# Moving one tile in 64 of a row gather from GpSimd to SyncE in a two-layer graph network

## What is computed

```
x_src = x[src]
msg   = sum over r of where(edge_type == r, x_src @ W[r], 0)
cnt   = zeros(nodes, 8).at[dst, edge_type].add(1)
norm  = 1 / max(cnt[dst, edge_type], 1)
out   = segment_sum(msg * norm, dst) + x @ root + bias
```

## Time and profile before

| | us |
|---|---|
| median of 3 runs | 19301.76 |
| lowest, highest | 19297.16, 19303.48 |
| the profiled execution, device time | 19300.3 |
| its span in the profile | 19298.5 |
| GpSimd busy | 13724.0 (71%) |
| TensorE busy, matmul / weight load | 8836.8 (46%) / 7749.4 (40%) |
| VectorE busy | 3708.6 (19%) |
| ScalarE busy | 2928.3 (15%) |

### The profile page before, as it was taken

One profiled execution on the slowest core, in us unless ns is written; L12 is line 12 of the kernel. 1 busy time (PEld: TensorE's weight loads), 2 busy tenths in 40 slices (PEclk: granted clock), 3 DMA queues, 4 the chain that ended last, 5 costly groups with the idle time before them and its releaser, 6 DMA issues. The chain is left out here.

```text
span 19298.5 us, 202733 instructions
## 1 busy us (share of the span) xinstructions
PE 8836.8 (46%) x35275; PEld 7749.4 (40%) x35276; DVE 3708.6 (19%) x4240; ACT 2928.3 (15%) x13902; POOL 13724.0 (71%) x14217
## 2 busy tenths in 40 slices
PE   6565054444544444544444444444544444444443
PEld 2343044444434443444434333433434434444433
DVE  2223921111111111111111211111111111111113
ACT  1001021111111111111111111111111111111111
POOL 1672977777777777777776577777777777777774
PEclk9556555555555555555555655555555555555555
DMA  2122010000000000000000300000000000000001
GB/s 82 53 53 93 15 14 7 7 7 7 7 7 7 7 7 7 7 7 7 7 7 6 66 7 7 7 7 7 7 7 7 7 7 7 7 7 7 7 7 10
DMA packets 659318, 296.37 MB, mean 15 GB/s; under 512 B 351570, under 2 KB 628327, under 8 KB 657917
## 3 DMA queue, kind: packets, MB, share of 16 engines
q0 software_dynamic: 455680, 168.10, 8.0%
q1 hardware_dynamic: 202813, 124.51, 2.6%
q10 hardware_dynamic: 402, 0.09, 0.0%
HBM read 207.97 MB, written 87.17 MB: 15 GB/s over the span
## 5 line engine op out<-in xcount | busy, mean ns | idle before, releaser
L109 POOL DMA_INDIRECT l_rows<-table,l_idx x13312 | 12854.8, 966 | 4628.7 <-issue 4056.0
L1002 PE MATMUL l_ps<-l_rows,l_hot 128*128 x28160 | 6327.3, 375 | 0.0
L1002 PEld LDWEIGHTS l_ps<-l_rows,l_hot 128*128 128x128 f32 x28160 | 6137.8, 330 | 395.1 <-issue 395.1
L999 PE MATMUL l_ps<-l_zero 1*128 1x128 f32 x3520 | 1341.0, 482 | 9041.2 <-issue 9041.2
L982 ACT ACTIVATE l_rows<-l_rows,all_big 128x16 f32<-128x16 f32 x13312 | 2662.7, 292 | 13759.6 <-DMA l_rows<-table,l_idx 13759.3
L999 PEld LDWEIGHTS l_ps<-l_zero 1*128 1x128 f32 x3520 | 873.9, 307 | 9179.8 <-issue 9179.8
L1035 DVE TENSOR_TENSOR all_big<-all_big,l_ps 128x128 f32 x1760 | 507.0, 288 | 13988.1 <-PE l_ps L1002 13988.1
L1041 DVE TENSOR_TENSOR l_hot<-l_ps,all_local 128x1024 f32<-128x1024 f32 x1760 | 2126.9, 1219 | 50.6 <-issue 49.9
L109 POOL DMA_INDIRECT s_rows<-table,s_idx x832 | 785.0, 944 | 320.8 <-issue 251.7
L520 PE MATMUL s_ps<-s_zero 1*128 1x512 f32 x448 | 345.1, 909 | 438.5 <-issue 390.0
L523 PEld LDWEIGHTS s_ps<-s_rows,s_hot 128*128 128x128 f32 x1792 | 373.1, 317 | 140.2 <-issue 140.2
(11 more groups left out here) (173 smaller groups left out, 1682.9 us busy)
## 6 DMA issues: line engine op xcount, KB each, us to landing
l_rows<-table,l_idx POOLq DMA_INDIRECT x13312, 2.3
table<-midt_out SPq DMA_DIRECT2D x49, 512.0 KB
table<-x1t_out SPq DMA_DIRECT2D x48, 512.0 KB, 2.7
table<-ed_out SPq DMA_DIRECT2D x48, 320.0 KB, 2.1
s_rows<-table,s_idx POOLq DMA_INDIRECT x832, 2.6
idx_d<-ed_typ SPq DMA_DIRECT2D x2, 3328.0 KB, 9.4
l_idx<-idx_d SPq DMA_DIRECT2D x208, 32.0 KB, 1.8
ed_typ<-in_edge_type_dram SPq DMA_DIRECT2D x2, 2912.0 KB
```

What stands on the lines that cost most here:

```text
L109: pool.indirect_dma_start(out=out[:, j, :], out_offset=None, in_=table, in_offset=bass.IndirectOffsetOnAxis(ap=idx[:, j:j + 1], axis=0)).t ...
L999: nc.tensor.matmul(sums[g % 2], zero[:, :], zero[:, :], start=True, stop=False, skip_group_check=True)
L1002: last = nc.tensor.matmul(sums[g % 2][:, bass.ds((v % GROUP) * FEAT, FEAT)], hot[:, g % 2, j, :], rows[:, bass.ds(v // GROUP, 1), :].rearr ...
```

## The change

It concerns the two runs of `stage_layer`. GpSimd gathers the first 63 tiles (`BY_POOL`) of each block of 64. The last tile's 128 rows are fetched by SyncE with 128 DMAs of one row (64 bytes) each. Their row numbers come from a small SBUF buffer `row_idx` of two halves, into which SyncE loads one column of `idx1_d` a block ahead; from there they are loaded into registers of SyncE, four at a time, with a minimum of 0 and a maximum of 399,999 (for layer 1; layer 2 has the same number). SyncE's part becomes `turn(i)`: turn 0 is written out ahead of the wait for `started`, turns 1 to 7 are a loop. In it the load of the next row numbers for the whole block stands behind the 128 row DMAs, and loads the list of block n + 12 once block n - 1 has landed. The rows of SyncE count on a semaphore of their own, `rows_in[b]`, and ScalarE waits for both. `idx1_d` gets 832 columns more, filled with the first ones again, so that loads ahead of the last turn have something to read.

```diff
--- before.py
+++ after.py
@@ -41,6 +41,8 @@
 GROUP = 8
 GROUPS = STEPS // GROUP
 RING = 13
+BY_SP = 1
+BY_POOL = SPAN - BY_SP
 RTILES = RING * SPAN
 TURNS = TILES // RTILES
 HOLD = -(-(WINS - 1 + SPAN - 1) // SPAN)
@@ -229,8 +231,9 @@
             sp.wait_ge(wide_read, batches)
             sp.dma_start(env.idx0_d, typ6[:, :]).then_inc(idx_out, 16)
             sp.wait_ge(wide_read, 2 * batches)
-            sp.dma_start(env.idx1_d, typ8[:, :]).then_inc(idx_out, 16)
-            sp.wait_ge(idx_out, 32)
+            sp.dma_start(env.idx1_d[:, TILES:], typ8[:, 0:RTILES]).then_inc(idx_out, 16)
+            sp.dma_start(env.idx1_d[:, 0:TILES], typ8[:, :]).then_inc(idx_out, 16)
+            sp.wait_ge(idx_out, 48)
             sp.wait_ge(tables_back, 96)
             sp.wait_ge(dst_stored, 48)
             for b in range(2):
@@ -922,6 +925,7 @@
         rows = s.sb("rows", [P, RTILES, FEAT])
         idx = s.sb("idx", [P, RING, SPAN], I32)
         hot = s.sb("hot", [P, 2, GROUP, P])
+        row_idx = s.sb("row_idx", [1, 2, P], I32)
         zero = s.sb("zero", [1, P])
         bias_in = s.sb("bias_in", [P, FEAT])
         ps = s.ps("ps", [P, 8 * 512])
@@ -930,32 +934,67 @@
                     "root_in", "other_in", "bias_added"))
         idx_in = [s.sem(f"idx_in{b}") for b in range(RING)]
         landed = [s.sem(f"landed{b}") for b in range(RING)]
+        rows_in = [s.sem(f"rows_in{b}") for b in range(RING)]
+        row_idx_in, rows_claimed = s.sem("row_idx_in"), s.sem("rows_claimed")
         norm = Norm(nc, env, s, ps) if first_layer else None
         sums = [ps[:, b * 512:b * 512 + GROUP * FEAT] for b in range(2)]
         lane_ps = ps[:, 2 * 512:2 * 512 + P]
         acc, root = env.acc, env.root
         per = SPAN // GROUP
+        table_rows = NODES1 * RELS
         by_node = lambda d: d.rearrange("(w n) f -> n w f", n=P)
         block = s.block()
 
         @block.sync
         def _(sp):
-            for b in range(RING):
-                sp.dma_start(idx[:, b, :], env.idx1_d[:, b * SPAN:(b + 1) * SPAN]).then_inc(idx_in[b], 16)
+            def load_idx(n, b):
+                at = bass.ds(n * SPAN, SPAN) if not isinstance(n, int) else slice(n * SPAN, (n + 1) * SPAN)
+                sp.dma_start(idx[:, b, :], env.idx1_d[:, at]).then_inc(idx_in[b], 16)
+
+            def load_row_idx(n, half):
+                at = bass.ds(n * SPAN + BY_POOL, 1) if not isinstance(n, int) else slice(
+                    n * SPAN + BY_POOL, (n + 1) * SPAN)
+                sp.dma_start(row_idx[:, half, :], env.idx1_d[:, at].rearrange("q a -> a q")).then_inc(row_idx_in, 16)
+
+            def turn(i):
+                for b in range(RING):
+                    n = i * RING + b
+                    half = n % 2 if isinstance(i, int) else bass.ds(n % 2, 1)
+                    sp.wait_ge(row_idx_in, 16 * (n + 1))
+                    load_row_idx(n + 1, (n + 1) % 2 if isinstance(i, int) else bass.ds((n + 1) % 2, 1))
+                    sp.wait_ge(free, n + 1)
+                    sp.sem_inc(rows_claimed, 1)
+                    for c in range(P // 4):
+                        _, where = nc.values_load_multi_w_load_instructions(
+                            row_idx[0:1, half, 4 * c:4 * c + 4], engines=[sp.engine],
+                            min_val=0, max_val=table_rows - 1)
+                        for j, v in enumerate(where):
+                            q = 4 * c + j
+                            sp.dma_start(rows[q:q + 1, b * SPAN + BY_POOL, :], table[bass.ds(v, 1), :]
+                                         ).then_inc(rows_in[b], 16)
+                    if isinstance(i, int) and n == 0:
+                        continue
+                    sp.wait_ge(landed[b - 1], (16 * BY_POOL) * ((i + 1) if b else i))
+                    load_idx(n + RING - 1, (b - 1) % RING)
+            for b in range(RING - 1):
+                load_idx(b, b)
+            load_row_idx(0, 0)
             if norm:
                 norm.sp(sp)
             sp.dma_start(bias_in[:, :], bias.rearrange("(a c) -> a c", a=1).to_broadcast([P, FEAT])
                          ).then_inc(root_in, 16)
+            load_idx(RING - 1, RING - 1)
+            turn(0)
             sp.wait_ge(started, 1)
             if first_layer:
                 sp.dma_start(root, by_node(env.root1_d)).then_inc(root_in, 16)
             else:
                 sp.dma_start(env.x1, by_node(env.x1_d)).then_inc(other_in, 16)
-            with sp.Fori(0, TURNS - 1) as i:
-                for b in range(RING):
-                    sp.wait_ge(landed[b], (i + 1) * (16 * SPAN))
-                    sp.dma_start(idx[:, b, :], env.idx1_d[:, bass.ds((i + 1) * RTILES + b * SPAN, SPAN)]
-                                 ).then_inc(idx_in[b], 16)
+            with sp.Fori(1, TURNS) as i:
+                turn(i)
+            for b in range(RING):
+                sp.wait_ge(idx_in[b], 16 * (TURNS + 1 if b < RING - 1 else TURNS))
+            sp.wait_ge(row_idx_in, 16 * (TURNS * RING + 1))
             if not first_layer:
                 sp.wait_ge(other_in, 16)
 
@@ -967,7 +1006,7 @@
                     pool.wait_ge(idx_in[b], (i + 1) * 16)
                     pool.wait_ge(free, i * RING + b + 1)
                     pool.sem_inc(claimed, 1)
-                    fetch(pool, rows[:, b * SPAN:(b + 1) * SPAN], table, idx[:, b], SPAN, landed[b])
+                    fetch(pool, rows[:, b * SPAN:(b + 1) * SPAN], table, idx[:, b], BY_POOL, landed[b])
 
         @block.scalar
         def _(act):
@@ -976,7 +1015,8 @@
                 act.wait_ge(norm.list_read, norm.batches)
             with act.Fori(0, TURNS) as i:
                 for b in range(RING):
-                    act.wait_ge(landed[b], (i + 1) * (16 * SPAN))
+                    act.wait_ge(landed[b], (i + 1) * (16 * BY_POOL))
+                    act.wait_ge(rows_in[b], (i + 1) * (16 * BY_SP * P))
                     for j in range(SPAN):
                         at = rows[:, b * SPAN + j, :]
                         last = nc.scalar.activation(at, at, ACT.Copy,
@@ -1156,7 +1196,7 @@
     dram = lambda name, shape, dt=F32: nc.dram_tensor(name, shape, dt, kind="Internal").ap()
     env.dst_d = dram("dst_d", (TILES * P,), I32)
     env.idx0_d = dram("idx0_d", (P, TILES), I32)
-    env.idx1_d = dram("idx1_d", (P, TILES), I32)
+    env.idx1_d = dram("idx1_d", (P, TILES + RTILES), I32)
     env.step_d = dram("step_d", (STEPS,), I16)
     env.step0_d = dram("step0_d", (STEPS,), I16)
     env.first_d = dram("first_d", (GROUPS,), I32)
```

## The result

The changed kernel takes 25,264.99 us (median of 4, 25,263.02 to 25,266.58) against 19,301.04 before: a ratio of 1.309 with an interval of 1.3067 to 1.3113, 31% slower. The profiled execution has a span of 25,261.6. The direction, the cause and the range of the prediction held; the time lies 2,475 us under the predicted 27,740.

A forecast was written before the change was run, and what follows sets the result against it. GpSimd's gather issue bounds the kernel before; SyncE's issue, 121.3 us a block against GpSimd's 78.6, was to bound the changed one. 2,387.6 + 208 x 121.3 + 125 = 27,743, about 27,740 us; range 24,200 to 30,000.

The forecast's parts named there:

- (a) Register load: SyncE's loads of row numbers, four registers at a time: 0.963 us per load, 0.27 us a row with arithmetic and gaps.
- (b) Bounds check: SyncE's register operation and assertion for each row number: 0.23 us a row, bounds 0.135 and 0.28.
- (c) Address: SyncE's register operation and move ahead of each row DMA: 0.15 us with gaps, upper bound 0.26.
- (d) The DMA: SyncE's issue of each single-row DMA: 0.29 us with the gap, lower bound 0.25.
- The rest of a block: SyncE's work per block besides the 128 rows (row-number column, index load, waits, counting): 1.6 us together.
- What waits: ScalarE, TensorE and VectorE run at SyncE's pace; GpSimd is held for index lists; `free` holds nobody.
- Fixed terms: Later starts, SyncE's wait in layer 1's slow gathers (28 us) and two bulk loads blocking its queue (76): sum 125 us.
- The first: Rival: SyncE is fast enough and GpSimd's 260 us is won, about 19,060 us; chance 0.05, 0.01 more for just balancing.
- the point of decision: SyncE's time per row at which the change would just balance: 80.7 us a block, 0.62 us a row.
- The second: Rival: SyncE's checks cost little or fall away, 0.71 us a row, 92.5 us a block, 21,750 us; chance 0.03.
- The third: Rival: the DMA queue limits, each row waiting for the previous landing, 232 us a block, 50,800 us; chance 0.04.
- The fourth: Rival: TensorE's instruction prices hold on SyncE, 1.16 us a row, 150 us a block, 33,700 us; chance 0.05.

The follow-up runs named there:

- run 1: Changed kernel without the run-time bounds check of SyncE's register loads: 19,055.52 us, ratio 0.9873 to the kernel before.
- run 2: Changed kernel without SyncE's register loads and row DMAs, last tile of each block left zero: 19,051.40 us, 0.9871 to the kernel before.
- run 4: Changed kernel, checks kept, 64 rows issued by SyncE and 64 by ScalarE's queue: 19,053.70 us, 0.9873 to the kernel before.
- run 3: Changed kernel with eight registers per load instead of four, checks kept: 23,840.32 us, 1.2352 to the kernel before.
- run 5: Changed kernel, TensorE's first two spans of each layer reading slot numbers from a 32-bit copy instead of the 16-bit table: 25,259.7 us.
- run 7: Changed kernel, no check, sixteen registers per load, two tiles per block taken from GpSimd, 144 rows by SyncE, 112 by ScalarE: 18,802.78 us, 0.9741 to before.
- run 6: Changed kernel with one register per load instead of four, checks kept: 36,793.71 us.
- run 8: Changed kernel with four single-register loads and their checks, then four row DMAs: 32,491.91 us.

## Why the prediction was right, and where it was off

**What bounds the kernel before** held: with one gather in 64 removed and nothing put in SyncE's way, runs 1, 2 and 4 gain 245 to 250 us, close to the 260 of the removed gathers. In the changed kernel layer 1 as a whole begins 9 us later, its first index load at 1,929.6 instead of 1,920.35. The only edit ahead of it is one more copy into `idx1_d`, which was not tried alone. The eight experiments have the same copy and begin at 1,923.4 (run 4) to 1,928.8 (run 1), so 6 of the 9 us lie within what these executions differ by.

**The new bound** held: 31% slower because SyncE's issue takes longer than the gathers beside it. The steps of a row:

- (a) Register load: **this is the term that failed.** I took 0.27 a row from a load of four at 0.963. It measures 0.466, so (0.466 + 0.051 + two gaps) / 4 = 0.15. The 0.231 for each further register came from a load of one 32-bit number and a load of eight 16-bit ones; it was no price of a register. For 32-bit numbers run 3 shows 0.057 on SyncE, and run 5 shows TensorE's load of eight fall to 0.592 with the width. Worth 0.12 x 128 x 208 = 3,200 us, more than the whole miss. The Trainium skill's 200 ns a register (Runtime: NRT & Kernel Launch, Instruction fetch mechanics), which I had set beside it, does not fit these loads from SBUF either: they take 117 ns a register in fours and 87 in eights.
- (b) Bounds check: 0.147 and 0.018 with gaps, 0.25, between SyncE's comparing row that I took (0.23) and TensorE's (0.28). Run 1 shows what it decides.
- (c) Address: 0.037 to 0.042 and 0.029, 0.14, as predicted (0.15).
- (d) The DMA: 0.225, and 0.26 for the first behind other work, 0.27 with the gap (0.29 predicted).

Together 0.82 instead of 0.94, and 105 instead of 120 us for 128 rows.

**The rest of a block** was too small: 1.6 predicted, about 4 measured (109.2 from block to block, less 105.2 for the rows). The column of row numbers costs 0.6 with 0.125 of arithmetic ahead, as costed. The largest thing that I had left out is the fetching of SyncE's code. The page's count for the instruction queue rose:

```profile
q14 instruction: 1560, 12.78, 0.2%
```

from 397 packets and 3.25 MB before. 9.5 MB more is what 146,600 more instructions make (349,337 less 202,733, 65 bytes each), 8 KB to a packet. In the trace of SyncE, between 4,000 and 6,000 us, a gap of 0.33 to 0.37 us instead of 0.04 stands every 128 instructions, and with some 22 instructions for four rows that is 5.7 times a block, 1.7 us, 350 us in the kernel. There are 103 such pauses in the stretch, and within 1 us behind each of them a packet of the instruction queue begins. On an idle SyncE it would not show. The Trainium skill (Runtime: NRT & Kernel Launch, Instruction fetch mechanics) calls the crossing from one block of code to the next mostly hidden, and its blocks are of 256 instructions; this trace has the pause at every 128, and on a sequencer at its limit it is not hidden. The first load of a block, behind the wait, adds another 0.2 us (0.65 instead of 0.466); some 0.5 us a block is not accounted for.

**What waits:** ScalarE's waits went over to the row DMAs, and TensorE and VectorE follow, as said. One detail was wrong without harm: I wrote that `free` holds nobody and that GpSimd would wait for index lists. It waits for `free` (L1056, 4,420 us in 147 waits): it runs ahead until the ring of 13 blocks is full, and that comes before the lists run out. The bound that I had given for `free` was for SyncE, which indeed never waits for it. GpSimd's two waits for index lists, 327 and 1,164 us, are those at the start of the two layers.

**Fixed terms:** the first row came at 1,952.2, 12 us later than I had it, 9 of them from the later begin of the layer. The bulk load held the queue for 39.2 us in layer 1 (the longest below) and 38.4 in layer 2:

```profile
L957 SPq DMA_DIRECT2D l_row_idx<-idx_d x210: 555/596/39177, 1935.2 to 24957.5; - x105
```

against 38 predicted from the earlier trace rows. The wait for GpSimd's slow stretch was 80 us and not 28, because a faster SyncE arrives at it earlier: with 109 us a block its fourth block ends at 2,384, and the third block of gathers lands at 2,464, as predicted (2,454) but for the layer's later begin. So the account is 208 x 109.2 + 80 + 2 x 39 = 22,872 for the two layers, against 22,877.6 in the trace.

**The rivals.** The first, a fast enough SyncE, is what runs 1 and 4 make of the kernel; the point of decision, 0.62 us a row, lies between run 1's 0.56 (its groups of four rows start 2.25 us apart) and the 0.82 of the change. I had thought that dropping the check alone would leave 0.71 and stay slower; with the right price of the load it leaves 0.56. The second, checks that cost little, fell with their 0.25. The third, the queue, fell with runs 1, 4 and 7, and the traces show it directly. Each row DMA has one packet of 64 bytes, which begins 0.6 us after the issue ended, and within 0.95 us in 99 of 100; this holds between 4,000 and 9,000 us of the changed kernel, of run 1 and, for both issuers, of run 7. So the rows did not queue up, even at one every 0.30 us (256 in 77.4). No row was split, but the trace does not name the DMA engines, so whether all rows went to the same one is not known.

The fourth, TensorE's prices, fell too: only the check comes near them. Its sum also took 0.30 for the address where the working had at most 0.26; with that it is 1.12 us a row and some 32,670 us.

## What to carry to other kernels

Before work goes to an idle sequencer, sum everything that it must issue per item, register loads, checks and address arithmetic included, and compare the sum with what it replaces; here the DMA itself was a third of the row's cost. Take each price from a row with the same width of numbers, the same number of registers and the same predecessor. If the sum is just too large, drop a redundant check or share the items between two sequencers: here each of these alone turned a loss of 31% into the gain that GpSimd's floor allows. Loading eight registers at once brought the loss down to 24%.

## What the hardware showed that I had not expected

- A register load of eight 16-bit numbers took 1.92 us, of eight 32-bit ones from a copy 0.59, on the same engine (run 5).
- SyncE's register load took 0.264 us for one register among register work but 0.436 where each stood behind a row DMA; behind a row DMA four took 0.466 and eight 0.692 (runs 6 and 8, the changed kernel, run 3). Behind an index load one took 0.27. Why it waits behind row DMAs is open.
- SyncE, running straight through long code, paused 0.3 us longer than usual every 128 instructions (the trace of the changed kernel).
- 256 row DMAs in 77 us from two sequencers, 64 bytes each, left GpSimd's gathers at 0.944 us and their own issue at 0.225 (SyncE) and 0.213 us (ScalarE), as with half as many (run 7).
